# Writing the column of maxima as fp32r and spreading it with fp32r products

## The reference

```python
q = (latents @ Wq)      # 32 heads of 128; latents = layernorm(x)
k = (kv @ Wk)           # 8 heads; kv = 1601 rows of context and the 256 latents, 1857 keys
v = (kv @ Wv)
q, k = rms_norm(q, q_norm_w), rms_norm(k, k_norm_w)
scores = jnp.einsum('bhgqd,bhkd->bhgqk', qg, k) * scale
probs = jax.nn.softmax(scores.astype(jnp.float32), axis=-1)
out = jnp.einsum('bhgqk,bhkd->bhgqd', probs, v)     # then @ Wo
```

## Time and profile before

| | |
|---|---|
| median of three runs | 3216.54 us |
| the profiled execution | 3211.71 us |
| its span, first to last instruction | 3209.9 us |
| TensorE busy | 3026.6 us, 94% of the span |
| weight loads | 2470.7 us, 77% |
| VectorE | 2455.7 us, 77% |
| ScalarE | 2052.9 us, 64% |
| GpSimd | 1317.7 us, 41% |
| attention, from the first of its transfers to its last product | about 256 to 2730 us |

### The profile page before, as it was taken

One profiled execution on the slowest core, in us unless ns is written; L12 is line 12 of the kernel. 1 busy time (PEld: TensorE's weight loads), 2 busy tenths in 40 slices (PEclk: granted clock), 3 DMA queues, 4 the chain that ended last, 5 costly groups with the idle time before them and its releaser, 6 DMA issues. The chain is left out here.

```text
span 3209.9 us, 52293 instructions
## 1 busy us (share of the span) xinstructions
PE 3026.6 (94%) x14906; PEld 2470.7 (77%) x14906; DVE 2455.7 (77%) x3316; ACT 2052.9 (64%) x2899; POOL 1317.7 (41%) x791
## 2 busy tenths in 40 slices
PE   6996999999899999998999999999999997697899
PEld 5884888888778888886788888778888885585577
DVE  6773888888958888887788888868888888423765
ACT  3443777777857777876787777767777786311211
POOL 1330455555525555555355555535555555000000
PEclk9998999999999999999999999999999998898899
DMA  6873110011211100012111010211011000734300
GB/s 227 274 234 117 33 40 33 33 41 41 75 35 33 47 33 33 33 37 85 34 33 42 33 39 33 73 47 35 33 37 45 33 26 11 218 100 132 96 30 20
DMA packets 183911, 210.92 MB, mean 66 GB/s; under 512 B 10965, under 2 KB 125653, under 8 KB 182761
## 3 DMA queue, kind: packets, MB, share of 16 engines
q1 hardware_dynamic: 179016, 196.27, 19.0%
q0 software_dynamic: 2176, 8.39, 0.8%
q10 hardware_dynamic: 2592, 4.72, 0.5%
HBM read 140.14 MB, written 69.21 MB: 65 GB/s over the span
## 5 line engine op out<-in xcount | busy, mean ns | idle before, releaser
L870 POOL TENSOR_TENSOR att_sm<-att_sm,att_sc 128x1024 f32<-128x1024 f32 (+1 forms) x384 | 852.6, 2220 | 697.0 <-DVE att_pr L821 696.5
L676 PE MATMUL att_ppv<-att_pr,att_V 128*128 128x512 f32 (+1 forms) x2880 | 848.8, 404 | 22.8 <-DVE att_pr L821 20.1
L656 PE MATMUL att_pqk<-att_q,att_kT 128*128 128x512 f32 (+1 forms) x2880 | 850.1, 404 | 6.6 <-issue 3.8
L748 ACT ACTIVATE att_sc<-att_pqk,att_rk 128x512 f32<-128x512 f32 (+1 forms) x960 | 661.8, 690 | 188.6 <-PE att_pqk L656 185.5
L617 PE MATMUL att_pkv<-att_ctxT,att_wkv 128*128 128x512 f32 (+1 forms) x3072 | 756.3, 376 | 1.1 <-DVE att_kT L837 0.5
L821 DVE TENSOR_TENSOR att_pr<-att_sc,att_pr 128x1024 fp32r<-128x1024 f32 (+1 forms) x512 | 631.7, 1234 | 37.8 <-ACT att_pr L759 37.8
L617 PEld LDWEIGHTS att_pkv<-att_ctxT,att_wkv 128*128 128x128 f32 x3072 | 559.5, 189 | 120.6 <-DVE att_kT L837 1.2
L676 PEld LDWEIGHTS att_ppv<-att_pr,att_V 128*128 128x128 f32 (+1 forms) x2880 | 532.6, 191 | 149.3 <-DVE att_pr L821 35.1
L815 DVE TENSOR_TENSOR att_sc<-att_sc,att_pmax 128x1024 f32<-128x1024 f32 (+1 forms) x512 | 585.2, 1143 | 42.7 <-PE att_pmax L625 42.7
L656 PEld LDWEIGHTS att_pqk<-att_q,att_kT 128*128 128x128 f32 (+1 forms) x2880 | 505.8, 185 | 122.5 <-ACT att_sc L748 14.1
L759 ACT CAST att_pr<-att_sc 128x1024 fp32r<-128x1024 f32 (+1 forms) x512 | 511.2, 998 | 137.3 <-PE att_ppv L676 135.8
(11 more groups left out here) (130 smaller groups left out, 2749.9 us busy)
## 6 DMA issues: line engine op xcount, KB each, us to landing
q_scr<-pre_qT SPq DMA_DIRECT2D x128, 256.0 KB, 3.5
att_wkv<-kv_scr SPq DMA_DIRECT2D x64, 512.0 KB, 4.0
att_q<-q_scr SPq DMA_DIRECT2D x64, 512.0 KB, 4.3
o_scr<-att_on SPq DMA_DIRECT2D x64, 256.0 KB, 2.0
out_oraw<-o_scr SPq DMA_DIRECT2D x64, 256.0 KB, 4.9
att_sc<-in_ctx SPq DMA_DIRECT2D x16, 768.0 KB, 4.7
pre_wq_raw<-in_L_xattn_Wq SPq DMA_DIRECT2D x8, 1024.0 KB, 6.8
kv_scr<-pre_kv SPq DMA_DIRECT2D x8, 1024.0 KB, 7.6
```

Of the source, the lines that this page charges most:

```text
L656: mm = pe.matmul(pqk[0:m, (h * NT + t) % 2], kT[:, kp, t * P:t * P + m], q[:, qp, h], start=(i == 0), stop=(i == 2))
L676: mm = pe.matmul(ppv[:], V[0:m, vp, t], pr[0:m, pp, (t // 2) % NP, t % 2], start=(t == 0 and i == 0), stop=(t == NT - 1 and i == 2))
L748: act.activation(sc[0:m, h, t], pqk[0:m, s % 2], ACT.Copy, scale=rk[0:m, t:t + 1]).then_inc(sc_ok, 1)
L870: pool.tensor_tensor(sm[0:m, 0:w], sm[0:m, 0:w], sc[0:m, h, i:i + w], ALU.add).then_inc(sum_ok, w)
```

## The change

`red` becomes a tile of fp32r, and so does what `tensor_reduce` writes into it. A second identity `identr` in fp32r is made by VectorE in the block that sets up the constants, after a wait for `ident`. `spread` takes the identity as an argument: `mb` gives it `identr`, `db` still `ident`.

```diff
-        red = sb("red", [P, 4])
+        red = sb("red", [P, 4], F32R)
+        identr = sb("identr", [P, P], F32R)
...
                 dve.memset(ones[:], 1.0).then_inc(cst_ok, 1)
+                dve.wait_ge(id_ok, 2)
+                dve.tensor_copy(identr[:], ident[:]).then_inc(cst_ok, 1)
                 dve.memset(vraw[:], 0.0).then_inc(cst_ok, 1)
...
-                def spread(bank, col):
+                def spread(bank, col, eye):
 
                     for c in range(4):
-                        mm = pe.matmul(bank[:, c * P:(c + 1) * P], col[:, c:c + 1].to_broadcast([P, P]), ident[:],
+                        mm = pe.matmul(bank[:, c * P:(c + 1) * P], col[:, c:c + 1].to_broadcast([P, P]), eye[:],
                                        start=True, stop=True)
                     return mm
...
-                        spread(pmax, red).then_inc(mb_ps, 1)
+                        spread(pmax, red, identr).then_inc(mb_ps, 1)
...
-                        spread(pred, rden).then_inc(db_ps, 1)
+                        spread(pred, rden, ident).then_inc(db_ps, 1)
```

## The result

The changed kernel takes 3191.75 us (median of five runs, 3188.03 to 3200.11), before 3215.82 us (median of five, 3212.68 to 3217.71): 24.1 us less, a ratio of 0.9931 with a 95% interval of 0.9915 to 0.9947. Measured again beside the experiments it was 3194.32 us against 3216.98, 0.9925 (0.9912 to 0.9939). The forecast was 3194.

The account below looks back on a forecast made before the run. The prediction took TensorE's issued work to bound the attention rounds. Spreads −24.9 us plus set-up +2.4 us gave −22.5 us: 3194 us from a median of 3216.54, own range 3188 to 3199, 8-in-10 range 3188 to 3220.

Parts of the forecast that it names:

- What bounds the kernel: Attention rounds: TensorE has no free time in 72.40 us, so its issued work sets the time; other engines have some 10 us slack.
- A pass costs a weight load: Maxima's spread on TensorE: loading 128 weight columns sets 0.111 us a pass; four passes instead of eight free 0.445 us.
- The lower bound: One fp32r pass of the spread, bounded by its stream: 0.45 ns a column, 0.061 us for 128 moving columns.
- The 56 spreads: Halves where VectorE's subtraction waits for the spread: each gains 0.445 us in full, 24.9 us together.
- The start: Set-up block: VectorE waits for GpSimd's identity, then copies it and does its memsets; +2.4 us, once.
- The 8 spreads at the ends of the batches: VectorE arrives after the spread without idle time and TensorE soon waits for it: counted as nothing, at best 3.6 us.
- The sum: Whole kernel: −24.9 + 2.4 = −22.5 us, giving 3189.2 us for the profiled execution and 3194 us on the median.
- A short fp32r product that costs two fp32 passes: Rival on the spread: fp32r no quicker, only the start's cost remains, 3219 us, or 3222 at 0.233 us a product; chance 0.20.
- A faster load: Rival on the spread: fp32r loads quicker, the stream sets 0.061 us a pass; 3183 to 3189 us; chance 0.07.
- the third rival: VectorE takes over in the rounds: only first halves count, 10.1 us gained, 3206 us; chance 0.08.
- The slow rival: Spread's fp32r loads no longer run under the product before: 1.86 us a spread, 54 us slower, 3273 us; chance 0.05.
- The rule of the Trainium skill: Spread's weight loads: 128 weights load faster when input is not FP32; a spread would then take 4 × 0.061 us.

## Why the prediction was right

*What bounds the kernel.* Right, and the rounds show it to 0.05 us: with one spread, both spreads and the sums of squares, TensorE has 8, 16 and 31 passes a round less, at 0.111 us each 0.89, 1.78 and 3.44 us, and a round is shorter by 0.89, 1.80 and 3.39 us (71.52, 70.61 and 69.02), without idle time before the products with V.

*A pass costs a weight load.* The step that rested on no row of its own, and it held: 0.44 us a spread for 0.445 forecast. The edits of weights, moving columns and count tell it apart from the others. The lower bound holds as well: I carried the stream down to 0.061 us, and with the load halved the passes started 0.059 us apart.

*The 56 spreads.* −24.9 us forecast, −25.2 in the 28 rounds.

*The start.* +2.4 us forecast, +2.4 measured, and 2.2 of it returned when the copy stood behind the memsets.

*The 8 spreads at the ends of the batches.* Counted as nothing, because TensorE would wait for VectorE soon after. For the first spread of a batch's last round the traces show that. TensorE's next wait for the low part, first in the kernel before, where the spread of rows 10 starts at 831.14, then in the changed one:

```profile
847.03 0.97 PE L676 MATMUL att_ppv<-att_pr,att_V 128*128 128x512 f32 x3 [0.27 <-DVE att_pr L821]
```

```profile
827.06 0.55 PE L628 MATMUL att_pmax<-att_identr,att_red 128*128 128x128 f32 x4
...
842.91 0.96 PE L679 MATMUL att_ppv<-att_pr,att_V 128*128 128x512 f32 x3 [0.69 <-DVE att_pr L824]
```

The wait ends 15.89 us after the spread's start before and 15.85 after: of the 0.45 us freed, 0.42 came back as waiting. The other two changes of batch have the same pair of waits, 0.27 and 0.67 to 0.68 us. For the second spread of such a round the term is neither shown nor refuted, since the changes of batch differ by far more than 0.45 us between executions of one program.

*The sum.* −22.5 us forecast; −24.1 and −22.7 in the two measurements. For the profiled execution itself I had worked out 3189.2 us, and it took 3194.47, 5.3 us more: the 4.3 us of the stretches other than the rounds and the set-up block, and 1.3 us more between the span and the time of the execution (3.1 us, before 1.8), less the 0.3 us that the rounds gained beyond the forecast. The sum of one profile is no better than that. That the median came out 2 us from the forecast is in part luck, since runs of the changed kernel lie between 3188 and 3200 us; the rounds and the start are what bears the account.

*The rivals.* A short fp32r product that costs two fp32 passes would have left the round at 72.41 us. A faster load would have shown 0.06 us a pass; the loads last 194 ns and the four passes take 0.44 us. VectorE does lose its last idle time before the subtraction in second halves, as the third rival said, but no wait on TensorE follows: VectorE had 10 us of slack elsewhere in the round, and a further 2.5 us a round could be taken from TensorE without using it up. The slow rival, 1.86 us a spread, is out by the same 0.44. The rule of the Trainium skill quoted ahead ("TensorE: Matmul & The Clock Gate", Weight-path perf modes), that loads of 128 weights are faster when the input is not FP32, does not show for fp32r here: 194 ns against 192 in fp32.

## What to carry to other kernels

Where TensorE sets the time, count a short product by its weight loads: with 128 columns of weights and up to 128 moving columns each took 0.11 us here, and plain fp32 pays it twice. The transposes do not, though they stand ahead among the plain fp32 products: those of the maxima, four for each of 64 halves, are one pass each in the trace of the changed kernel, and nothing can be halved there.

```profile
L666 PE MATMUL att_pred<-att_ident,att_mx 128*128 128x128 f32 x256 | 39.4, 277 | 8.2 <-DVE att_on L836 8.2
```

If the numbers stand rounding to fp32r, find all helpers that pay twice, not one: the two spreads and the sums of squares together, with the copy moved, brought 3.2%, the one spread 0.7%. And put an instruction that waits for another engine behind those that don't, even in a block of constants that runs once.

## What the runs showed that was not expected

Halving the weight columns of the spread gave a round 0.28 us where 0.4 were expected, though the passes came as close as forecast, 0.059 us: 0.05 us of what a spread costs lies in the products behind it, which kept their own weights. And the same instructions at the start of the attention took 60.6 to 65.1 us at a granted clock of 0.92 to 0.83, more of a difference than two of the edits tried here make.
